# The tails of two graph convolutions: the first one's values made with nodes on the partitions, the second one's two activations of neighbouring chunks interleaved

## The chip, the cores and the metric

The kernel runs on one core of one Trainium2 chip. The metric is the time of one execution on the device, in microseconds (us).

## The reference, cut to what matters

The program is a graph network of four layers on 6,250 nodes and 106,250 edges (each layer: layer norm, ReLU, a graph convolution, added to x). The change touches only the third layer, in which a small network of its own computes a correction t for every node:

```python
h = jnp.ones((N, 1), x.dtype)
h = jax.nn.elu(spline_conv(h, row, col, basis, idx, stn1_w, stn1_b))   # [N, 64]  first convolution
h = jax.nn.elu(spline_conv(h, row, col, basis, idx, stn2_w, stn2_b))   # [N, 64]  second convolution
h = jax.nn.elu(h @ stn3_w + stn3_b)                                    # [N, 64]
t = h @ stn4_w + stn4_b                                                # [N, 3]
...
# spline_conv ends: out = segment_sum(msg); deg = segment_sum(1)
return out / jnp.maximum(deg, 1.0)[:, None] + b
```

Since the first convolution's input is all ones, its sum is one matrix product per node: the summed basis (125 values of a node) times stn1_w [125, 64]. ELU is computed as max(v, 0) + exp(min(v, 0)) - 1.

## The kernel before, in words

The kernel is a chain of phases. Each is a Block in which five instruction streams (SP, PE, ACT, DVE, POOL; that is SyncE, TensorE, ScalarE, VectorE, GpSimd) run side by side and wait for each other on semaphores. A Block ends when every stream has drained and met the others (in the trace: DRAIN and EVENT_SEMAPHORE on the Block's line), and `next_phase()` (L100) adds one more barrier. Nothing of the next phase starts earlier, its DMAs included. Nodes are 49 blocks (NB) of 128 nodes, grouped in 7 chunks (NCH) of 7 blocks; CHUNK is 896 nodes, HALF is 448. All tensors here are float32. PSUM is `ps`, 8 banks of 512 float32 on each partition.

**First tail.** `source_order_pass` (L1581, Block at L1617) goes over 880 tiles of 128 edges. For each tile POOL sends one indirect DMA (L1729) that scatters 128 records of 208 float32 into the DRAM table `rec_d`, from a ring of UB = 10 slots of G = 4 tiles; ACT fills a slot only when its last scatters have landed (L1699). PE and DVE sum the 125 basis values and a count of each node into `acc` [126, 6272], node along the free axis, the count in row 125. When the loop is done, POOL still has the ring to send and then waits for its landings (L1733). Beside that, the functions of `job_post_spline` (L1457) make the first convolution's values, one chunk after the other: PE multiplies `wt` and the selector `sel` (all ones in its row 125) with the chunk (two `product` calls, bank pairs 0 and 2), so that features lie on 64 partitions and the count is repeated on all of them; DVE takes max(count, 1) (L1507), its reciprocal (L1508), the quotient (L1509), and the two halves of ELU (`elu_of`, L1450 and L1451); ACT takes Exp (L1488); DVE adds up (L1453); PE turns the seven [64, 128] pieces so that nodes lie on partitions (L1306, bank 4); ACT copies them to `nodes` (L1491), and only then lets PE begin the next chunk (`s_out`). The `val`, `rc`, `low` and `hid` tiles are lent from the pass's `oh` and `basis`.

**Next phase.** `destination_order_pass` (L1883) begins with loads of weights (L2559) and of `rec_d` (L1910), the table that POOL has just filled.

**Second tail.** `post_stn` (L1514, Block at L1524) is a phase of its own, in which POOL issues nothing. Its input `rows` has nodes on the partitions. For each chunk in turn: PE turns seven blocks (L1537, into banks 0 and 1), DVE, ACT and DVE make ELU (L1450, L1451, L1559, L1453, into `hid`), PE multiplies by w3 (L1293, banks 4 and 5), DVE, ACT and DVE make ELU again into `hid2`, PE multiplies by w4 (L1552, bank 6), and DVE adds the last bias into `nodes` (L1577). There is one `low`, one `hid` and one `hid2`; PE turns the next chunk beside the second ELU.

Of the kernel before, what the change touches and what calls it, by code (L numbers as in the profile page):

```python
# [82 lines left out]
def build(nc, A, out, debug=None):  # L83
    ctx = ExitStack()
    with ctx:
# [574 lines left out]
        def column(ap):  # L660
            return ap.rearrange("(o a) -> o a", a=1)
# [785 lines left out]
        def elu_of(v, then, low, s_low, s_exp):  # L1447

            def elu(e, x, view, b, to, sem):
                nc.vector.tensor_scalar(view(low[:, :]), x, b, 0.0, ALU.add, ALU.min).then_inc(s_low, 1)  # L1450
                then(nc.vector.tensor_scalar(view(to[:, :]), x, b, 0.0, ALU.add, ALU.max))  # L1451
                v.wait_ge(s_exp, e + 1)
                nc.vector.scalar_tensor_tensor(out=to[:, :], in0=low[:, :], scalar=-1.0, in1=to[:, :],  # L1453
                                               op0=ALU.add, op1=ALU.add).then_inc(sem, 1)
            return elu

        def job_post_spline(c, acc, count_row, w1, b1, nodes, lent):  # L1457

            H = 64
            wt, bt = weight(c, "wt", count_row, H), weight(c, "bt", H, 1)  # L1460
            sel = weight(c, "sel", count_row + 1, H)
            rc, val, low, hid = lent
            s_w, s_z, s_mm, k, s_low, s_exp, s_hid, s_tr, s_out = (sem_in(c, n) for n in (
                "weights", "selector", "products", "chain", "low", "exp", "hid", "turned", "out"))
# [6 lines left out]
            def pe_start(pe):  # L1471
                pe.wait_ge(s_w, 32)
                pe.wait_ge(s_z, 1)
                nc.tensor.sem_inc(s_out, 1)

            def pe_chunk(pe, ch):
                pe.wait_ge(s_out, ch + 1)
                nc.tensor.sem_inc(tick, 1)
# [3 lines left out]
                nc.tensor.sem_inc(tick, 1)  # L1482
                turn(4, hid, H, s_tr)

            def act_chunk(act, ch):
                act.wait_ge(s_low, ch + 1)
                nc.scalar.sem_inc(tick, 1)
                nc.scalar.activation(low[:, :], low[:, :], ACT.Exp).then_inc(s_exp, 1)  # L1488
                act.wait_ge(s_tr, ch + 1)
                nc.scalar.sem_inc(tick, 1)  # L1490
                nc.scalar.copy(nodes[:, ds(ch * 7 * H, 7 * H)], ps[:, 4, 0:7 * H]).then_inc(s_out, 1)  # L1491

            def dve_start(v):
                select_row(c, sel[:, :], count_row).then_inc(s_z, 1)
                v.wait_ge(s_w, 32)

            def dve_chunk(v, ch):
                at = [0]

                def then(ins):  # L1500
                    at[0] += 1
                    ins.then_inc(k, 1)
                    v.wait_ge(k, 4 * ch + at[0])

                v.wait_ge(s_mm, ch + 1)
                nc.vector.sem_inc(tick, 1)
                then(nc.vector.tensor_scalar(split(rc[:, :]), halves(2, H), 1.0, None, ALU.max))  # L1507
                then(nc.vector.reciprocal(rc[:, :], rc[:, :]))  # L1508
# [5 lines left out]
        def post_stn(rows, b1, w_in, b_in, w_out, b_out, nodes):  # L1514

            H = 64
            with ExitStack() as c:
# [6 lines left out]
                with nc.Block() as block:  # L1524
# [9 lines left out]
                    def _(pe):  # L1534
# [1144 lines left out]
```

## Time and profile before

| what | value |
|---|---|
| time before, median of 3 runs | 11786.78 us (11779.63 to 11808.97) |
| the profiled execution | 11795.48 us, of which 11793.6 us are the span of the trace |
| POOL busy | 6775.0 us (57%) |
| PE, weight loads, DVE, ACT busy | 52%, 41%, 47%, 19% |
| TensorE clock granted, mean | 0.584 of full speed |

No engine is busy throughout: the phases have different limits, and a phase must be read by itself. In the rows below an instruction is given as: engine, line, operation, out<-in, form. "PEld" is the weight load of PE. A name with q (POOLq, SPq) is the engine's sequencer or DMA queue. The granted clock is a share of 2.4 GHz: 0.50 is the lower of its two levels, 1.2 GHz. A float32 matmul stands as two passes in the trace (the seven of L1552 are x14).

### The profile page before, as it was taken

What the parts mean: (1) busy time and instruction counts of PE and PEld (TensorE: products, weight loads), DVE (VectorE), ACT (ScalarE), POOL (GpSimd) and SP (SyncE); (2) the same over time, 40 slices, a digit from 0 to 9 for tenths busy, and PEclk for the clock granted to TensorE, in tenths of its full rate; (3) what the DMA queues carried; (4) which work ended last, traced back from release to release, by engine and by line L of the source; (5) the groups of instructions that cost most, each with busy time, mean ns of one, the idle gap of its engine ahead of it and who ended that gap; (6) DMA issues with size and microseconds to landing.
All of it is one profiled execution on the core that took longest, in us unless ns stands there. A gap on an engine that the chain in (4) does not pass through costs nothing. (4 is left out here: it accounts for less than half of the span.)

```text
span 11793.6 us, 174145 instructions
## 1 busy us (share of the span) xinstructions
PE 6097.0 (52%) x42047; PEld 4878.5 (41%) x42048; DVE 5490.5 (47%) x10617; ACT 2204.9 (19%) x6466; POOL 6775.0 (57%) x6936
## 2 busy tenths in 40 slices
PE   5200166665777756665534435555554555643535
PEld 1100045554777644445323324244444444432424
DVE  9200175555555578876734335721113333543425
ACT  0000034442333311110031220011111111122030
POOL 0777547774777767773462350067777777445070
PEclk9555587776555578875555555755555555555555
DMA  9940012222333311116744345580000111134454
GB/s 369 169 46 5 23 52 83 83 83 72 104 104 104 87 46 54 54 47 93 109 167 111 122 135 117 102 69 14 14 13 20 28 28 27 36 106 137 97 177 95
DMA packets 1401293, 1002.71 MB, mean 85 GB/s; under 512 B 950077, under 2 KB 1243772, under 8 KB 1383486
## 3 DMA queue, kind: packets, MB, share of 16 engines
q1 hardware_dynamic: 1006396, 578.07, 22.8%
q0 software_dynamic: 246144, 278.83, 7.7%
q10 hardware_dynamic: 148608, 144.19, 4.2%
q8 instruction: 54, 0.88, 0.0%
q14 instruction: 91, 0.74, 0.0%
HBM read 494.76 MB, written 546.25 MB: 88 GB/s over the span
## 5 line engine op out<-in xcount | busy, mean ns | idle before, releaser
L2500 POOL DMA_INDIRECT msg<-msg,idx x1792 | 1743.1, 973 | 592.9 <-issue 531.7
L976 POOL DMA_INDIRECT run_rows<-rec,idx x1088 | 1065.2, 979 | 1232.6 <-ACT rec L960 992.3
L2330 POOL DMA_INDIRECT cell<-rec,idx x944 | 931.3, 987 | 1007.6 <-ACT rec L2318 725.1
L665 DVE TENSOR_TENSOR oh<-iota_f,rd 128x512 bf16<-128x512 f32 (+1 forms) x1181 | 775.6, 690 | 1280.4 <-PE ps L2252 1015.3
L2052 POOL DMA_INDIRECT cell<-rec,idx x936 | 973.3, 1040 | 401.3 <-issue 284.6
L1729 POOL DMA_INDIRECT rec_d<-rec,idx x880 | 904.0, 1027 | 453.5 <-issue 267.0
L396 POOL DMA_INDIRECT rec_r<-sc_rec,sc_idx x832 | 816.4, 981 | 587.9 <-ACT sc_rec L387 307.0
L946 PE MATMUL ps<-planes,hot 128*128 x4352 | 474.9, 294 | 979.2 <-ACT rec L960 852.2
L931 DVE TENSOR_SCALAR hot<-loc,lane_c 128x512 bf16<-128x512 bf16 x1088 | 406.3, 387 | 958.4 <-PE ps L946 892.2
L946 PEld LDWEIGHTS ps<-planes,hot 128*128 128x128 bf16 x4352 | 363.8, 135 | 1090.7 <-issue 1042.6
L2480 PE MATMUL ps<-w_stn,hft 128*128 x1792 | 597.1, 491 | 405.3 <-ACT hft L2434 396.8
L2267 PE MATMUL ps<-h_rows,oht 128*128 x1888 | 450.9, 403 | 540.1 <-ACT oht L2274 539.7
L1042 PE MATMUL ps<-got,oh 128*128 128x33 bf16 x11328 | 561.7, 197 | 312.1 <-DVE oh L665 297.7
L2480 PE MATMUL ps<-w_conv,hft 128*128 x1792 | 436.8, 425 | 501.7 <-ACT hft L2434 501.7
L271 PE MATMUL ps<-mark,column 128*128 128x416 bf16 (+2 forms) x454 | 117.3, 375 | 1101.8 <-DVE mark L202 1096.1
L2267 PEld LDWEIGHTS ps<-h_rows,oht 128*128 128x128 f32 x1888 | 420.3, 327 | 633.6 <-issue 633.6
L2404 DVE TENSOR_REDUCE msg<-wy 128x256 f32<-128x1024 f32 (+1 forms) x448 | 525.8, 1174 | 274.2 <-DMA msg<-msg,idx 258.3
L1042 PEld LDWEIGHTS ps<-got,oh 128*128 128x128 bf16 x11328 | 483.5, 108 | 387.6 <-issue 332.5
L2480 PEld LDWEIGHTS ps<-w_conv,hft 128*128 128x128 f32 x1792 | 396.9, 326 | 587.8 <-issue 587.7
L2480 PEld LDWEIGHTS ps<-w_stn,hft 128*128 128x128 f32 x1792 | 414.5, 242 | 534.2 <-issue 465.5
L1970 PE MATMUL ps<-h,oht 128*128 x1872 | 459.0, 427 | 292.2 <-ACT rec L2034 292.2
L1759 PE MATMUL ps<-xgs,oht 128*128 x2640 | 402.7, 299 | 349.2 <-ACT rec L1674 348.8
(419 smaller groups left out, 13675.7 us busy)
## 6 DMA issues: line engine op xcount, KB each, us to landing
loc<-loc_s SPq DMA_DIRECT2D x136, 1024.0 KB
got<-run_rows SPq DMA_DIRECT2D x944, 112.0 KB
got<-rec_d SPq DMA_DIRECT2D x234, 416.0 KB
rec_d<-padd ACTq DMA_DIRECT2D x4, 12480.0 KB
rec_d<-padd ACTq DMA_DIRECT2D x4, 12064.0 KB
cin<-cell SPq DMA_DIRECT2D x224, 136.0 KB, 2.1
loc<-loc_d SPq DMA_DIRECT2D x236, 128.0 KB
cell<-rec,idx POOLq DMA_INDIRECT x1880
```

Of the source, the lines that this page charges most:

```text
L396: nc.gpsimd.indirect_dma_start(out=table, out_offset=bass.IndirectOffsetOnAxis(ap=s["idx"][:, n, g:g + 1], axis=0), in_=s["rec"][:, n, g, ...
L665: return nc.vector.tensor_tensor(oh, bcast(iota_f[:, :].unsqueeze(1), [P, G, P]), bcast(local.unsqueeze(2), [P, G, P]), ALU.is_equal)
L946: mm = nc.tensor.matmul(ps[:, m % RING, g * W:(g + 1) * W], hot[:, m % RING, g * P:(g + 1) * P], flat[:, ds(ids[m % HU] * W, W)], start=Tr ...
L976: nc.gpsimd.indirect_dma_start(out=out, out_offset=bass.IndirectOffsetOnAxis(ap=idx[:, u, m % HU:m % HU + 1], axis=0), in_=rec[:, m, :], i ...
L1042: mm = nc.tensor.matmul(sums[:, ds(at[n * G + g], AW)], oh[:, n, g, :], part[n][:, g, q * AW:(q + 1) * AW], start=False, stop=False)
L1729: nc.gpsimd.indirect_dma_start(out=rec_d, out_offset=bass.IndirectOffsetOnAxis(ap=idx[:, n, g:g + 1], axis=0), in_=rec[:, n, g, :], in_off ...
L2052: nc.gpsimd.indirect_dma_start(out=cells, out_offset=bass.IndirectOffsetOnAxis(ap=idx[:, n, g:g + 1], axis=0), in_=rec[:, n, g, :], in_off ...
L2267: mm = nc.tensor.matmul(ps[:, 2 + n % 2, g * W:(g + 1) * W], s["oht"][:, n % 2, g, :], nodes[:, ds(ids[g] * pitch, W)], start=True, stop=True)
L2330: nc.gpsimd.indirect_dma_start(out=cells, out_offset=bass.IndirectOffsetOnAxis(ap=idx[:, n, g:g + 1], axis=0), in_=rec[:, n, g, :], in_off ...
L2404: nc.vector.tensor_reduce(msg[:, n, :, 0:F], wy[:, n % 2, :, :, :].rearrange("p g c o -> p g o c"), AX.X, ALU.add).then_inc(s_msg, 1)
L2480: mm = nc.tensor.matmul(ps[:, 2 + banks * (n % 2) + col // 512, col % 512:col % 512 + rest * F], hft[:, n % 2, g, :], w, start=True, stop= ...
L2500: nc.gpsimd.indirect_dma_start(out=msgs, out_offset=bass.IndirectOffsetOnAxis(ap=idx[:, n, g:g + 1], axis=0), in_=msg[:, n, g, :], in_offs ...
```

## The change

In the first tail the stationary and the moving operand are exchanged: `acc` [126, 128 nodes] is loaded as the weights and one matrix `w_cnt` [126, 65] is moved, which holds stn1_w in columns 0 to 63 and a one for the count row in column 64. A block's result [128 nodes, 65] fills 65 columns of a bank, seven blocks fill a bank, and each of the seven chunks has a bank of its own (0 to 6). The count is then one column: max and reciprocal are taken of [128, 7]. The bias is added as a row `b_row`, loaded to all 128 partitions. Nothing is turned, and ACT copies nothing. PE waits for nobody between chunks; DVE makes the value of chunk q + 1 before it ends ELU of chunk q. The three streams are written out instead of looped. At the start of the phase SP's two small loads wait for DVE's memset of `w_cnt`, and DVE makes the selector column after these loads have landed.

In the second tail there are two `low` and two `hid`; PE turns chunk 1 at once and chunk ch + 2 after the product of chunk ch; DVE makes the first ELU of chunk ch + 1 between the parts of the second ELU of chunk ch.

```diff
         def job_post_spline(c, acc, count_row, w1, b1, nodes, lent):
             H = 64
-            wt, bt = weight(c, "wt", count_row, H), weight(c, "bt", H, 1)
-            sel = weight(c, "sel", count_row + 1, H)
-            rc, val, low, hid = lent
+            W = H + 1
+            w_cnt, b_row, rc = weight(c, "w_cnt", count_row + 1, W), sb_in(c, "b_row", [P, H]), sb_in(c, "rc", [P, NB])
+            low = [x.rearrange("p (b f) -> p b f", f=H) for x in lent]
+            def value(q):
+                return nodes[:, q * 7 * H:(q + 1) * 7 * H].rearrange("p (b f) -> p b f", f=H)
             def loads_sp(sp):
-                sp.dma_start(bt[:, :], column(b1)).then_inc(s_w, 16)
-                sp.dma_start(wt[:, :], w1).then_inc(s_w, 16)
+                sp.wait_ge(s_z, 1)
+                sp.dma_start(w_cnt[0:count_row, 0:H], w1).then_inc(s_w, 16)
+                sp.dma_start(b_row[:, :], bcast(b1.unsqueeze(0), [P, H])).then_inc(s_w, 16)
                 sp.wait_ge(s_w, 32)
-            def pe_chunk(pe, ch):
-                pe.wait_ge(s_out, ch + 1)
-                product(0, H, [(wt[:, :], moving(acc, count_row, ch))])
-                product(2, H, [(sel[:, :], moving(acc, count_row + 1, ch))], s_mm)
-                pe.wait_ge(s_hid, ch + 1)
-                turn(4, hid, H, s_tr)
-            def act_chunk(act, ch):
-                act.wait_ge(s_low, ch + 1)
-                nc.scalar.activation(low[:, :], low[:, :], ACT.Exp).then_inc(s_exp, 1)
-                act.wait_ge(s_tr, ch + 1)
-                nc.scalar.copy(nodes[:, ds(ch * 7 * H, 7 * H)], ps[:, 4, 0:7 * H]).then_inc(s_out, 1)
+            def pe_all(pe):
+                pe.wait_ge(s_w, 32)
+                pe.wait_ge(s_z, 2)
+                for q in range(NCH):
+                    for j in range(7):
+                        b = q * 7 + j
+                        mm = nc.tensor.matmul(ps[:, q, j * W:(j + 1) * W], acc[0:count_row + 1, b * P:(b + 1) * P], w_cnt[:, :],
+                                              start=True, stop=True)
+                    mm.then_inc(s_mm, 1)
+            def act_all(act):
+                for q in range(NCH):
+                    act.wait_ge(s_low, q + 1)
+                    nc.scalar.activation(low[q], low[q], ACT.Exp).then_inc(s_exp, 1)
             def dve_start(v):
-                select_row(c, sel[:, :], count_row).then_inc(s_z, 1)
+                nc.vector.memset(w_cnt[:, :], 0.0).then_inc(s_z, 1)
                 v.wait_ge(s_w, 32)
-            def dve_chunk(v, ch):
-                ...
-                then(nc.vector.tensor_scalar(split(rc[:, :]), halves(2, H), 1.0, None, ALU.max))
-                then(nc.vector.reciprocal(rc[:, :], rc[:, :]))
-                then(nc.vector.tensor_tensor(split(val[:, :]), halves(0, H), split(rc[:, :]), ALU.mult))
-                elu_of(v, then, low, s_low, s_exp)(ch, val[:, :], lambda a: a, bt[:, 0:1], hid, s_hid)
+                select_row(c, w_cnt[:, H:W], count_row).then_inc(s_z, 1)
+            def dve_all(v):
+                def mean(q):
+                    got = ps[:, q, 0:7 * W].rearrange("p (b f) -> p b f", f=W)
+                    mine = rc[:, q * 7:(q + 1) * 7]
+                    v.wait_ge(s_mm, q + 1)
+                    then(nc.vector.tensor_scalar(mine, got[:, :, H], 1.0, None, ALU.max))
+                    then(nc.vector.reciprocal(mine, mine))
+                    then(nc.vector.tensor_tensor(value(q), got[:, :, 0:H], bcast(mine.unsqueeze(2), [P, 7, H]), ALU.mult))
+                    then(nc.vector.tensor_tensor(value(q), value(q), bcast(b_row[:, :].unsqueeze(1), [P, 7, H]), ALU.add))
+                    nc.vector.tensor_scalar(low[q], value(q), 0.0, None, ALU.min).then_inc(s_low, 1)
+                def elu(q):
+                    then(nc.vector.tensor_scalar(value(q), value(q), 0.0, None, ALU.max))
+                    v.wait_ge(s_exp, q + 1)
+                    then(nc.vector.scalar_tensor_tensor(out=value(q), in0=low[q], scalar=-1.0, in1=value(q), op0=ALU.add, op1=ALU.add))
+                mean(0)
+                for q in range(NCH):
+                    if q + 1 < NCH:
+                        mean(q + 1)
+                    elu(q)
...
         def post_stn(rows, b1, w_in, b_in, w_out, b_out, nodes):
-                low, hid, hid2 = (sb_in(c, n, [H, CHUNK]) for n in ("low", "hid", "hid2"))
+                low, hid = ([sb_in(c, f"{n}{q}", [H, CHUNK]) for q in range(2)] for n in ("low", "hid"))
+                hid2 = sb_in(c, "hid2", [H, CHUNK])
...
                         turn_rows(0)
+                        pe.wait_ge(s_top, 1)
+                        turn_rows(1)
                         for ch in range(NCH):
                             pe.wait_ge(s_hid, ch + 1)
-                            product(4, H, [(w3[:, :], still(hid, H))], s_m3)
-                            if ch + 1 < NCH:
-                                turn_rows(ch + 1)
+                            product(4, H, [(w3[:, :], still(hid[ch % 2], H))], s_m3)
+                            if ch + 2 < NCH:
+                                pe.wait_ge(s_top, ch + 2)
+                                turn_rows(ch + 2)
                             pe.wait_ge(s_h3, ch + 1)
...
-                        for ch in range(NCH):
-                            v.wait_ge(s_turn, ch + 1)
-                            elu(2 * ch, flat, lambda a: a, bt[:, 0:1], hid, s_hid)
-                            v.wait_ge(s_m3, ch + 1)
-                            elu(2 * ch + 1, halves(4, H), split, b3[:, 0:1], hid2, s_h3)
-                            v.wait_ge(s_m4, ch + 1)
+                        def begin(e, to, x, view, b, top):
+                            nc.vector.tensor_scalar(view(e[:, :]), x, b, 0.0, ALU.add, ALU.min).then_inc(s_low, 1)
+                            nc.vector.tensor_scalar(view(to[:, :]), x, b, 0.0, ALU.add, ALU.max).then_inc(top, 1)
+                        def end(e, to, n, sem):
+                            v.wait_ge(s_exp, n)
+                            nc.vector.scalar_tensor_tensor(out=to[:, :], in0=e[:, :], scalar=-1.0, in1=to[:, :],
+                                                           op0=ALU.add, op1=ALU.add).then_inc(sem, 1)
+                        def first(ch):
+                            v.wait_ge(s_turn, ch + 1)
+                            begin(low[0], hid[ch % 2], flat, lambda a: a, bt[:, 0:1], s_top)
+                        first(0)
+                        v.wait_ge(s_top, 1)
+                        end(low[0], hid[0], 1, s_hid)
+                        for ch in range(NCH):
+                            more = ch + 1 < NCH
+                            if more:
+                                v.wait_ge(s_hid, ch + 1)
+                                first(ch + 1)
+                            if ch:
+                                keep(ch - 1)
+                            v.wait_ge(s_m3, ch + 1)
+                            v.wait_ge(s_h3, ch)
+                            begin(low[1], hid2, halves(4, H), split, b3[:, 0:1], k3)
+                            if more:
+                                v.wait_ge(s_top, ch + 2)
+                                end(low[0], hid[(ch + 1) % 2], 2 * ch + 2, s_hid)
+                            v.wait_ge(k3, ch + 1)
+                            end(low[1], hid2, 2 * ch + 3 if more else 2 * ch + 2, s_h3)
+                        keep(NCH - 1)
```

`keep(ch)` is the wait for w4's product and the addition that stood at L1576 and L1577. `w_cnt` is one tile; `select_row` (L1316) is unchanged.

## Rows read from the trace of the kernel before

**Rows 1.** The profile page: busy time of each engine.
```profile
...
PE 6097.0 (52%) x42047; PEld 4878.5 (41%) x42048; DVE 5490.5 (47%) x10617; ACT 2204.9 (19%) x6466; POOL 6775.0 (57%) x6936
```

**Rows 2.** Windows of the tails: us, busy of PE, PEld, DVE, ACT, POOL, clock, DMA.
```profile
...
2715.40:2847.10 131.70, 45.84 (x105) 16.81 (x105) 72.11 (x42) 10.38 (x14) 36.60 (x37) 0.63 0.03 9
5824.30:5925.00 100.70, 56.21 (x175) 33.99 (x175) 50.85 (x54) 14.58 (x15) 0.00 (x0) 0.50 0.00 0
```

**Rows 3.** Groups by line and form, 2715 to 2848 us.
```profile
...
L1508 DVE RECIPROCAL oh<-oh 64x896 f32<-64x896 f32 x7 | 40.2, 5745 | 0.2
...
L1450 DVE TENSOR_SCALAR basis<-oh,bt 64x896 f32<-64x896 f32 x7 | 4.7, 678 | 0.3
```

**Rows 4.** Timeline of the first tail: start, length, instruction, idle before it.
```profile
...
2715.44 3.25 PE L1293 MATMUL ps<-acc,wt 125*64 x4 [2.38 <-PEq L1474]
...
2732.21 1.25 POOL L1729 DMA_INDIRECT rec_d<-rec,idx  x1 [0.30 <-issue]
...
2762.19 0.97 POOL L1729 DMA_INDIRECT rec_d<-rec,idx  x1 [0.30 <-issue]
...
2846.52 0.53 ACT L1491 COPY h<-ps 128x448 f32 x1 [2.51 <-PE ps L1306]
2847.99 11.05 SPq L2559 DMA_DIRECT2D w_stn<-in_L_gnn_stn_w  x2
```

**Rows 5.** Sequencer events of the block at L1617 (ns: least, median, most).
```profile
...
L1617 POOLq EVENT_SEMAPHORE  x2: 17/17/17, 2847.1 to 2847.2; - x2
...
L1617 POOLq DRAIN  x1: 6601/6601/6601, 2764.5 to 2764.5; - x1
```

**Rows 6.** The POOL drain of three other blocks.
```profile
...
L2361 POOLq DRAIN  x2: 5287/5288/5290, 5311.1 to 10089.2; - x2
...
L2289 POOLq DRAIN  x1: 9208/9208/9208, 8925.2 to 8925.2; - x1
...
L569 POOLq DRAIN  x1: 19164/19164/19164, 1390.5 to 1390.5; - x1
```

**Rows 7.** Nearest instructions elsewhere: two of DVE by source, then PE and DVE by timeline.
```profile
...
L1439 DVE RECIPROCAL rc<-rc x3: 465/466/466, 4145.7 to 10448.1; 128x49 f32<-128x49 f32 x3
...
L1822 DVE TENSOR_TENSOR basis<-pair,hats x220: 678/679/745, 1582.8 to 2689.1; 128x500 f32<-128x500 f32 x110
...
6555.46 3.25 PE L1365 MATMUL ps<-v,hid 64*128 64x64 f32 x14
...
6558.64 1.75 PE L1293 MATMUL ps<-both_t,w 64*64 64x448 f32 x2
...
1572.17 5.29 DVE L1865 MEMSET acc<- 126x6272 f32 x1 [4.77 <-issue]
```

**Rows 8.** Window where L1365 ran.
```profile
...
6550.00:6600.00 50.00, 49.32 (x152) 29.59 (x153) 6.48 (x23) 11.95 (x13) 0.00 (x0) 0.50 0.00 0
```

**Rows 9.** Timeline of the second tail: its first chunk, and its last output.
```profile
...
5829.82 1.70 PE L1537 MATMUL ps<-ident,sums 128*64 128x128 f32 x7 [9.55 <-DMA b<-in_L_gnn_stn_b]
...
5832.71 1.13 DVE L1451 TENSOR_SCALAR hid<-ps,bt 64x896 f32<-64x896 f32 x1
...
5833.87 1.08 DVE L1453 SCALAR_TENSOR_TENSOR hid<-low,hid 64x896 f32<-64x896 f32 x1
...
5835.01 3.24 PE L1293 MATMUL ps<-hid,w 64*64 64x448 f32 x4 [3.49 <-DVE hid L1453]
...
5838.29 1.14 DVE L1450 TENSOR_SCALAR low<-ps,b 64x896 f32<-64x896 f32 x1 [3.33 <-PE ps L1293]
...
5840.53 1.08 DVE L1453 SCALAR_TENSOR_TENSOR hid<-low,hid 64x896 f32<-64x896 f32 x1
...
5841.66 3.15 PE L1552 MATMUL ps<-w,hid 64*128 64x4 f32 x14 [1.78 <-DVE hid L1453]
5844.85 0.19 DVE L1577 TENSOR_TENSOR t_nm<-ps,b 128x28 f32<-128x28 f32 x1 [3.24 <-PE ps L1552]
...
5924.66 0.18 DVE L1577 TENSOR_TENSOR t_nm<-ps,b 128x28 f32<-128x28 f32 x1 [3.23 <-PE ps L1552]
```

More of the change, by code:

```diff
@@ L1445, in _ @@
                         then(nc.vector.tensor_tensor(x_nm[:, :, :], x_nm[:, :, :], val, ALU.add))
[L1447 to L1455, printed above, removed]
@@ L1512, in job_post_spline @@
-            return dict(sp=loads_sp, pe_start=pe_start, pe_chunk=pe_chunk, act_chunk=act_chunk, dve_start=dve_start, dve_chunk=dve_chunk)
+                select_row(c, w_cnt[:, H:W], count_row).then_inc(s_z, 1)
+            def dve_all(v):
+                then = chain(v, k)
+                def mean(q):
[16 more added lines that the diff above has]
+                    elu(q)
@@ L1557, in _ @@
                         for e in range(2 * NCH):
+                            to = low[0 if e == 0 or (e % 2 == 1 and e < 2 * NCH - 1) else 1]
                             act.wait_ge(s_low, e + 1)
-                            nc.scalar.activation(low[:, :], low[:, :], ACT.Exp).then_inc(s_exp, 1)
+                            nc.scalar.activation(to[:, :], to[:, :], ACT.Exp).then_inc(s_exp, 1)
                     @block.vector
@@ L1569, in _, with keep @@
                         v.wait_ge(s_w, 80)
-                        elu = elu_of(v, then, low, s_low, s_exp)
-                        for ch in range(NCH):
+                        def begin(e, to, x, view, b, top):
[6 more added lines that the diff above has]
+                        def first(ch):
                             v.wait_ge(s_turn, ch + 1)
-                            elu(2 * ch, flat, lambda a: a, bt[:, 0:1], hid, s_hid)
-                            v.wait_ge(s_m3, ch + 1)
-                            elu(2 * ch + 1, halves(4, H), split, b3[:, 0:1], hid2, s_h3)
+                            begin(low[0], hid[ch % 2], flat, lambda a: a, bt[:, 0:1], s_top)
+                        def keep(ch):
                             v.wait_ge(s_m4, ch + 1)
@@ L1602, in source_order_pass @@
                      "basis", "summed", "added", "filled", "consts", "away"))
-                room = [x[0:64, :, :, :].rearrange("p r g w -> p (r g w)") for x in (oh, basis)]
-                post = job_post_spline(c, acc, KW, w1, b1, nodes,
-                                       [x[:, h * CHUNK:(h + 1) * CHUNK] for x in room for h in range(2)])
+                room = [x[:, :, :, :].rearrange("p r g w -> p (r g w)") for x in (oh, basis)]
+                post = job_post_spline(c, acc, KW, w1, b1, nodes, [room[q // 4][:, q % 4 * HALF:(q % 4 + 1) * HALF] for q in range(NCH)])
                 shift = {-4.0: 0, 1.0: 1, -3.0: 2, 2.0: 3, -2.0: 4, 4.0: 5}
@@ L1717, in _ @@
                         spans(act, body)
-                        with act.Fori(0, NCH) as ch:
-                            post["act_chunk"](act, ch)
+                        post["act_all"](act)
                     @block.gpsimd
@@ L1778, in _ @@
                         pe.wait_ge(s_fill, NT * UB + 2)
-                        post["pe_start"](pe)
-                        with pe.Fori(0, NCH) as ch:
-                            post["pe_chunk"](pe, ch)
+                        post["pe_all"](pe)
                     @block.vector
@@ L1879, in _ @@
                         v.wait_ge(s_cast, NT * UB)
-                        with v.Fori(0, NCH) as ch:
-                            post["dve_chunk"](v, ch)
+                        post["dve_all"](v)
         def destination_order_pass(rd, acc, nodes, F, cells, load_weights):
```

23 lines of the change are left out of this document (5 added, 18 removed).

## The prediction

> **What bounds the kernel now.** I read the page first: no engine is busy throughout, and the largest share, GpSimd's 57%, is an average over phases [rows 1]. So the question is which stream ends each of the two phases that the change touches. The windows give the stakes [rows 2]: the first tail is 131.7 us long, the second phase 100.7 us, and no engine is busy for more than 72 of the one or 56 of the other. Both are chains of waits. Together they are 232.4 us, 2.0% of the time, and no more than that is at stake.
>
> *First tail.* The timeline has PE's first product at 2715.44 and ACT's last copy at 2846.52 [rows 4]; seven chunks in series, 18.8 us each. The groups say what fills a chunk: the reciprocal of 896 elements on 64 partitions, 5.745 us, is the largest piece [rows 3]. But another stream runs beside it. POOL sends its ring until 2762.19 [rows 4], and the Block's events tell how that stream ends: its last wait is over and its DRAIN begins at 2764.5, and this DRAIN lasts 6.60 us, to 2771.1 [rows 5]. Now that is hidden: the last stream arrives, and POOL's event of the barrier follows, at 2847.1 [rows 5]. The reader is to see that POOL's drain is the floor of this phase, and that it lies 76.0 us below the present end.
>
> *Second tail.* One chunk by the timeline [rows 9]: product 5835.01, min 5838.29, last part of ELU 5840.53, w4's product 5841.66, bias 5844.85; the last bias at 5924.66 is (5924.66 - 5844.85) / 6 = 13.30 us per chunk. PE waits while DVE and ACT make an ELU, and DVE while PE multiplies. POOL issues nothing there, so no floor lies near.
>
> **First tail, part by part.** Removed for each chunk: the product with the selector, DVE's 5.745 us reciprocal, seven turns, ACT's copy (0.53 us), and PE's wait for it. Added:
>
> - PE: seven float32 matmuls of 65 columns on loads of 128, 14 passes. The nearest row is L1365, 64 columns on 64 rows, 14 passes in 3.25 us, with the next product 3.18 us after its start, where the granted clock was 0.50, the lower level [rows 8]. Seven chunks: 22.3 us. They wait for nobody.
> - DVE: max of [128, 7] and its reciprocal, at most the 0.47 us that 49 elements took [rows 7] each; a product, an addition and L1453's operation over 448 elements, at most 0.68 us each, what 500 elements took [rows 7]; min and max over 448, at most the 0.68 us that 896 took [rows 3]. Upper sum 0.94 + 2.04 + 1.36 = 4.3 us. Scaled to 448 elements and 7, it is about 0.3 + 1.8 + 0.7 = 2.8 us. I add 0.4 for chained waits and take 3.2 us, the same as PE's.
>
> So DVE's last chunk ends at about 2715.4 + 7 x 3.2 + 3.5 = 2741, at the upper bound 2715.4 + 3.2 + 7 x 4.3 = 2749. Both are before 2764.5. What ends the phase is POOL. The gain stops at POOL's floor, and PE's and DVE's exact costs are then worth nothing, as long as a chunk takes less than (2771.1 - 2718.6) / 7 = 7.5 us.
>
> What the change does to POOL itself: in the first chunk one scatter lasted 1.25 us instead of 0.97, beside DVE's last ELU operation [rows 4], and there was one such scatter in each of the two full chunks before POOL ended. I take that as DVE holding POOL up, 0.28 us for about 2.4 us of DVE work that has two SBUF inputs or runs at the fast rate (L1450's 0.68 us for 896 [rows 3], L1451 the same, L1453's 1.08 us). The new code has some 1.9 us of that in each of seven chunks, 13.3 us: 13.3 x 0.28 / 2.4 = 1.6 us, less the 0.56 us that go, is +1.0 us. Bounds: 0, and all 13.3 us. *The Trainium skill, SBUF — State Buffer, section "Who interferes with whom", calls the ports that the two engines share an exclusive lock which blocks the loser for the whole instruction, for tensor_scalar in its fast mode and for two SBUF inputs. The rows agree in kind, with 0.28 us of 1.08. By the rule in full the sum would be 12.3 us worse; it is a rival below.*
>
> The drain: 6.60 us here, with as many scatters and as large ones after the change. Elsewhere it lasted 5.29, 9.21 and 19.16 us [rows 6], so it is no constant; I keep 6.60, bounds 5.29 and 19.16. At the head of the phase the selector column now follows the loads (the wait behind which DVE's memset of `acc` stands is 4.77 us [rows 7]): about 0.1 us later for it, and everything of this POOL-paced pass is behind it. The bias load writes 128 rows instead of 64; I cost it at nothing, up to 0.5 us. POOL's end: 2771.1 + 1.0 + 0.1 = 2772.2. Gain 2847.1 - 2772.2 = **74.9 us**. The next phase's loads, issued 0.9 us after the barrier [rows 4, 5], move up with it. They need POOL's table, so could not have started earlier.
>
> **Second tail.** The same instructions in another order. Per chunk, from the start S of the operation that completes `hid2` [rows 9]: w4's product at S + 1.13; the w3 product of the next chunk is now ready and follows on PE 3.18 us later [rows 7], S + 4.31; min of its result 3.28 us later, S + 7.59; max, then the two closing additions at 2.24 us and one more operation of 1.08 us behind: S + 7.59 + 2.24 + 1.08 = S + 10.9. First ELU, turns and the bias lie inside PE's 6.4 us. So 10.9 us against 13.30. The ends: in chunk 0 PE makes the second turn first (it starts at 5833.9 when max is ready, and lasts 1.7 us [rows 9]), which puts the product 0.6 us later, and the added first-ELU operation 1.08 us more: S(1) is 5840.53 + 1.6 = 5842.1. Five periods of 10.9, then a last one without the next chunk's operation, 9.8: S(7) = 5906.5 and the last bias 4.32 us behind (5844.85 - 5840.53), 5910.8. Gain 5924.66 - 5910.8 = **13.9 us**. Bounds: 0.5 us per period either way, 11 and 17. PE's share: its 6.4 us per period are at the lower clock, 0.50 [rows 2].
>
> **Sum.** 74.9 + 13.9 = 88.8 us. The profiled execution took 11795.48 us: 11706.7. It stands 8.7 us above the median of the runs shown; against that median, 11786.78 - 88.8 = **11698 us**, 0.75% faster. A change under 0.3% (35 us) could not be told from none.
>
> **Rivals.**
>
> 1. *The drain shrinks or stretches* when it alone ends the phase. A POOL that issued nothing drains at once, and the rows with scatters spread from 5.29 to 19.16 [rows 6]. 19.16 gives 11711 us. *The Trainium skill, VectorE: DVE Perf Modes, section "The DRAIN you can't avoid", tells of DRAINs of about 12 ns on all engines at the ends; were POOL's that short with nothing behind it, the time would be 11691 us.* The rows speak against it: in four blocks with scatters, none under 5.2 [rows 5, 6]. Chance 0.08 for the long one, 0.03 for none.
> 2. *DVE locks POOL out in full*: 12.3 us more, 11710 us. For: the scatter of 1.25 us [rows 4]. Against: it was 0.28 us per chunk so far. Chance 0.07.
> 3. *DVE's chunk stays the end of the first tail*, a chunk over 7.5 us, because chained small operations cost more than the rows show. At 10 us a chunk the end is 2789: 11715 us. Chance 0.04.
> 4. *TensorE's clock rises in the second tail*, since it is busy 56 of 87 us instead of 101. Products would take half: about 2.7 us less per chunk, 11682 us. Against: where L1365 stands PE was busy for 49.3 of 50 us and the clock was 0.50 [rows 8]. Chance 0.04.
> 5. *The interleaving gives nothing*, because PE's turn or a wait falls into the period: 11712 us. Chance 0.04.
> 6. *Slower.* The head of the phase: DVE's memset of `acc` stands behind the loads, which now wait for DVE first and of which one is a broadcast to 128 partitions. POOL paces the pass, so each microsecond there is paid in full. The wait is 4.77 us now [rows 7]; it decides from 89 us on; at twice that, 178 us, the time would be 11876. Nothing among the rows is near. Chance 0.02. In between, at no measurable change: 0.03.
>
> The forecast has what is left, 0.65, with 11688 to 11706 us from its bounds and the spread of the runs before (7 us below the median, 22 above). The range reaches from rival 4's side to past rivals 1, 2, 3 and 5: 11681 to 11720. Faster by over 0.3%: 0.95; same 0.03; slower 0.02.
>
> **What would show it.** In the first tail: POOL's DRAIN on the Block's line is the last and the barrier follows it at about 2772; DVE's last closing addition lies near 2741, 14 passes of PE take about 3.2 us; scatters over 0.97 us are few. In the second: 10.9 us from w4's product to w4's product, the last bias 86 to 87 us after the phase's begin instead of 100.4. Wrong would make it: another stream than POOL last in the first, a drain far from 6.6, or later phases that give back what comes early.

## The result, and the profile after

The changed kernel takes 11734.55 us (median of 6 runs, 11720.64 to 11748.36), the kernel before 11807.06 us (median of 6 runs on the same chip, 11779.63 to 11813.3; the first three of them had the median 11786.78 that the prediction used). The ratio is 0.9945, 95% interval 0.9931 to 0.9958: 0.55% or 72.5 us faster. The prediction had 11698 us, a range to 11720, and a gain of 88.8 us. The measured time lies outside the range. The profiled execution took 11736.98 us, of which 11734.4 are the span, 59.2 less than the span of before.

Both tails first. Timeline of the first tail after:

```profile
...
2708.08 20.01 PE L1470 MATMUL ps<-w_cnt,acc 126*128 126x65 f32 x98 [1.78 <-DVE acc L1887]
...
2710.31 0.17 DVE L1491 TENSOR_SCALAR rc<-ps 128x7 f32<-128x7 f32 x1 [2.29 <-PE ps L1470]
...
2717.77 1.15 POOL L1758 DMA_INDIRECT rec_d<-rec,idx  x1 [0.31 <-issue]
...
2732.83 0.63 DVE L1500 SCALAR_TENSOR_TENSOR h<-basis,h 128x448 f32<-128x448 f32 x1
...
2755.26 0.97 POOL L1758 DMA_INDIRECT rec_d<-rec,idx  x1 [0.30 <-issue]
2765.09 9.84 SPq L2585 DMA_DIRECT2D w_stn<-in_L_gnn_stn_w  x2
```

Sequencer events of its block (ns: least, median, most):

```profile
...
L1647 POOLq EVENT_SEMAPHORE  x2: 17/17/17, 2764.2 to 2764.3; - x2
...
L1647 PEldq DRAIN  x1: 4070/4070/4070, 2724.1 to 2724.1; - x1
L1647 ACTq DRAIN  x1: 604/604/604, 2731.4 to 2731.4; - x1
...
L1647 DVEq DRAIN  x1: 17/17/17, 2733.7 to 2733.7; - x1
...
L1647 POOLq DRAIN  x1: 6601/6601/6601, 2757.6 to 2757.6; - x1
```

The seven chunks that took PE and ACT until 2846.52 [rows 4] are done by DVE 25.4 us after PE's first product. DVE's drain begins at 2733.7, but the barrier comes at 2764.2: 2757.6 + 6.60. POOL is now the last stream, and its drain has the length of before to the nanosecond [rows 5]. The first product of w4 to the last, and the last bias, in the second tail after:

```profile
...
5793.40 3.15 PE L1552 MATMUL ps<-w,hid 64*128 64x4 f32 x14 [2.66 <-DVE hid L1578]
...
5796.48 3.24 PE L1293 MATMUL ps<-hid,w 64*64 64x448 f32 x4
...
5799.76 1.14 DVE L1573 TENSOR_SCALAR low<-ps,b 64x896 f32<-64x896 f32 x1 [2.99 <-PE ps L1293]
...
5801.89 2.07 DVE L1578 SCALAR_TENSOR_TENSOR hid<-low,hid 64x896 f32<-64x896 f32 x2
...
5804.01 3.15 PE L1552 MATMUL ps<-w,hid 64*128 64x4 f32 x14 [2.66 <-DVE hid L1578]
...
5846.47 3.15 PE L1552 MATMUL ps<-w,hid 64*128 64x4 f32 x14 [4.29 <-DVE hid L1578]
```

From product to product it is 10.61 us, against the 13.30 of before [rows 9]. PE's clock stayed where it was. Windows of the first tail and of the whole second phase, with columns as in rows 2:

```profile
...
2708.00:2764.30 56.30, 20.01 (x98) 19.82 (x98) 20.93 (x50) 4.04 (x7) 36.95 (x38) 0.51 0.08 22
...
5774.60:5859.90 85.30, 55.81 (x175) 34.02 (x175) 50.01 (x54) 14.57 (x15) 0.00 (x0) 0.50 0.00 1
```

The lengths of phases can be read from POOL's barrier events on each Block's line, as in rows 5. All that differ by over 2.5 us between the two profiled executions:

| phase | before, us | after, us | difference |
|---|---|---|---|
| source pass with the first tail | 1280.9 | 1203.6 | -77.3 |
| second tail | 100.7 | 85.3 | -15.4 |
| sum of messages and ids (scatters of L1123) | 321.0 | 357.3 | +36.3 |
| third of four phases at L1006 | 245.1 | 253.2 | +8.1 |
| a phase before the pass (L569) | 1105.6 | 1101.0 | -4.6 |
| L2289 before, L2315 after | 1239.2 | 1235.4 | -3.8 |
| first phase at L912 | 371.9 | 369.3 | -2.6 |

The rest adds up to 0.1. The two tails gave 92.7 us; what is missing was given back later, in phases whose source did not change. For the largest piece there is one row, a single scatter (the 114th of 236) that lasted 38.89 us where its neighbours last 0.97:

```profile
...
5534.59 0.97 POOL L1123 DMA_INDIRECT run_ids<-acc_nm  x1 [0.30 <-issue]
5545.02 38.89 POOL L1123 DMA_INDIRECT run_ids<-acc_nm  x1 [9.46 <-issue]
5584.22 0.97 POOL L1123 DMA_INDIRECT run_ids<-acc_nm  x1 [0.30 <-issue]
```

Before, the longest of the same 236 took 1.50 us:

```profile
...
L1123 POOL DMA_INDIRECT run_ids<-acc_nm x236: 971/976/1499, 5475.5 to 5791.9; - x118
```

The idle time of about 9 us ahead of it is no part of the loss: before, 9.12 us stand at the same place. POOL ends this phase, so the long scatter counts; DVE, the next stream, is through 34 us earlier, so without it the phase would have been some 35 us shorter, not 38:

```profile
...
L2209 DVEq DRAIN  x1: 17/17/17, 5710.0 to 5710.0; - x1
...
L2209 POOLq DRAIN  x1: 876/876/876, 5744.4 to 5744.4; - x1
```

The +8.1 us are spread over the 59 turns of a loop. The window of that phase and DVE's main group, before and after (the columns of a group are busy us, mean ns | idle us before):

```profile
...
10848.00:11093.10 245.10, 142.15 (x2840) 121.83 (x2840) 154.22 (x241) 0.00 (x0) 0.00 (x0) 0.50 0.55 111
...
L665 DVE TENSOR_TENSOR oh<-iota_f,rd 128x512 bf16<-128x512 f32 x236 | 151.9, 688 | 85.3 <-PE ps L1042 85.2
```

```profile
...
10779.30:11032.50 253.20, 150.28 (x2840) 122.35 (x2840) 149.96 (x241) 0.00 (x0) 0.00 (x0) 0.50 0.53 107
...
L665 DVE TENSOR_TENSOR oh<-iota_f,rd 128x512 bf16<-128x512 f32 x236 | 147.7, 687 | 97.8 <-PE ps L1042 97.5
```

The counts and the granted clock are the same, and no DVE operation is longer. DVE waits 12.3 us more for PE, and PE's busy time is 8.1 us longer at the same number of matmuls. So PE's stream itself runs slower. The starts of the single matmuls in the trace show that it does so at one place of its code: a turn of the loop has 48 matmuls of L1042, and from the start of the 5th to that of the 6th it is 118 ns on average where it was 28, and from the 6th to the 7th 112 where it was 44; the first 12 matmuls of the 59 turns took 34.3 us in all instead of 26.2, the other 36 as long as before within 1 us. What had changed for PE was only where its code lies: in the built program its stream has 14,347 instructions instead of 14,195, and the 152 new ones all stand ahead of this phase.

### The profile page after: what moved, and what is told of

The parts are those of the page before. It is cut to its first block and busy times, and to the rows that moved or that the text cites. A ratio compares the mean times of both kernels' runs of the same rounds, so it can differ in the third digit from the quotient of the medians.

```text
span 11734.4 us, 174003 instructions
## 1 busy us (share of the span) xinstructions
PE 6071.7 (52%) x42040; PEld 4886.1 (42%) x42041; DVE 5431.0 (46%) x10625; ACT 2195.1 (19%) x6459; POOL 6800.9 (58%) x6936
## 5 line engine op out<-in xcount | busy, mean ns | idle before, releaser
L1042 PE MATMUL ps<-got,oh 128*128 128x33 bf16 x11328 | 571.0, 197 | 313.8 <-DVE oh L665 297.6
L1042 PEld LDWEIGHTS ps<-got,oh 128*128 128x128 bf16 x11328 | 486.3, 109 | 396.0 <-issue 339.4
```

The costliest lines, as they stand in the source:

```text
L1042: mm = nc.tensor.matmul(sums[:, ds(at[n * G + g], AW)], oh[:, n, g, :], part[n][:, g, q * AW:(q + 1) * AW], start=False, stop=False)
```

## The experiments

The kernel before, which took 11,807 us in the first timing, takes 13,433 us beside e1 to e4 (chip number 15 on record), 13,426 beside e5 to e8 (number 5), 13,583 beside e9 to e12 (number 7) and 13,559 beside e13 to e16 (number 5 again). Below, "the first chip" is that of the first timing, and "the other chips" are these. But the number 5 stands for two times that are 1% apart, and the first chip has no number on record: whether the chip itself or another condition of a timing makes the difference is not shown. Each run has the ratio to the kernel before that was timed beside it. Phase lengths come from one profile each. For the length of the source pass, three profiles of the changed kernel's pass at 13,560 to 13,580 us give 1469.2, 1473.2 and 1474.7, so a few microseconds there mean nothing; those of the third L1006 phase agree within 1 us.

**Kernel before, and kernel after, once more.**

> The kernel before, unchanged, for a second profile. In the first pair of profiles the two changed phases gained 77.4 and 15.4 us, but the phase that sums the messages (Block at L2183) grew by 36.2 us, with one POOL scatter of L1123 that lasted 38.89 us. Theory A (the long scatter comes by chance, in either kernel): the source pass is 1281 us and the second tail 100.7 us long again, while the phase at L2183 can be 321 or some 355 us here as well; some of the executions lie 30 us and more above others. Theory B (the change brings the long scatter about, by where it puts the phase in time or its code in memory): 321 us here, and no scatter of L1123 above 2 us.

> The changed kernel, unchanged, for a second profile. Both theories: source pass 1203.6 us, second tail 85.3 us. Theory A: the phase that sums the messages is 321 us as often as 357, and over enough executions the gain is near 92 us. Theory B: 357 us again, one scatter of L1123 near 39 us at the same place in its row of 236, and the gain stays near 72 us.

e1: 13434.85 us, ratio 1.0001 (0.9991 to 1.0011). e2: 13325.5, 0.9913 (0.9896 to 0.9929), 107.7 us faster. The source pass went from 1553.2 to 1447.5 us (-105.7), which is more than on the first chip, and the second tail from 100.8 to 85.6. The third L1006 phase lasted 253.3 instead of 244.3 us: this loss is there again. No scatter of L1123 was longer than 2.5 us.

The source pass ends in another way on these chips. Events of the block in e2:

```profile
...
L1647 POOLq DRAIN  x1: 6601/6601/6601, 3037.0 to 3037.0; - x1
...
L1647 DVEq DRAIN  x1: 17/17/17, 3060.6 to 3060.6; - x1
```

POOL is through at 3043.6, and DVE at 3060.6 sets the end. The groups of POOL over the pass tell why, first in the changed kernel on the first chip, then in e2:

```profile
...
L1758 POOL DMA_INDIRECT rec_d<-rec,idx x880 | 902.1, 1025 | 453.4 <-issue 267.1 <-ACT rec L1704 186.3
```

```profile
...
L1758 POOL DMA_INDIRECT rec_d<-rec,idx x880 | 913.1, 1038 | 676.1 <-ACT rec L1704 425.3 <-issue 250.8
```

On the first chip 185.4 of the 186.3 us that POOL waits for ACT stand before the first scatter; then it hardly waits, and the ring is nearly full when the pass's loop ends: 38 scatters follow. In e2 192.9 of 425.3 us stand before the first, and 232 us of waiting fall into the pass: the ring is nearly empty at the end, and so POOL has no backlog behind which seven chunks could hide: it sends its last scatter 5.3 us after PE's first product, against 47.2 us on the first chip. On these chips the gain is not cut at POOL's floor.

**Each tail alone.** e3 is the changed kernel with `post_stn` as before, e4 the kernel before with the new `post_stn`.

> Only the first tail changed, post_stn as before. Both theories: source pass 1204 us (77 us less), second tail 100.7 us, so 77 us faster without the message phase. Theory B, if the first tail is what brings the long scatter about: 77 - 36 = 41 us faster than before, with the scatter near 39 us; if not, 77. Theory A: 77 us, or 41 by chance.

> Only the second tail changed (post_stn), the first as before. It runs after the phase with the long scatter, so it can bring it about only by the layout of the code. Both theories: source pass 1281 us, second tail 85.3 us, 15.4 us less. Theory B by layout: the long scatter here too, 15 - 36 = 21 us slower than before. Theory A: 15 us faster, give or take the chance.

e3: 13342.68 us, 0.9926 (0.9909 to 0.9942), -90.5; source pass 1449.5, second tail 100.8, third L1006 phase 252.8. e4: 13416.74, 0.9984 (0.9974 to 0.9993), -16.5; 1553.0, 85.3, 243.4. The two add up to 107.0, and both together gave 107.7. The loss in the L1006 phase comes with the first tail's change alone, which stands ahead of that phase by some 8,000 us and has no code in it.

**PE's code put back, all streams' code put back.** e5 adds PE instructions that do nothing but count, behind the new products: 152 and 104 make 256, so that the later code lies where it lay before, modulo 256 instructions:

```diff
                         post["pe_all"](pe)
+                        for _ in range(104):
+                            nc.tensor.sem_inc(tick, 1)
```

e6 does so for every stream: 201 such increments on DVE, 8 on ACT, 8 on POOL, 6 on SP.

> The changed kernel with 104 semaphore increments added on PE behind its products of the first tail. The change made PE's code 152 instructions longer; with these it is 256 longer, so all later code of PE lies at the old place modulo 256 instructions. In every profile with the new first tail the summing phase that is third of four (Block at L1006) took 253 us, in every one with the old tail 243.4 to 245. Theory L (layout of PE's code): 245 us again, the rest as in the changed kernel, so 8 us faster than it. Theory T (it is the data, the time or another stream that moved): 253 us. The increments cost PE about 5 us behind POOL's scatters and the phase nothing.

> The same for all five streams: the increments bring the later code of PE and DVE to 256 instructions behind the old place, and that of ACT, POOL and SP to the old place. Theory L': layout of DVE's or another stream's code counts: 245 us here, and 253 in the run with PE's alone. Theory L: 245 us in both. Theory T: 253 us in both. With layout as before, the gain over the kernel before should be the two tails' own: 77 + 15 = 92 us where POOL ends the source pass.

e5: 13323.21 us, 0.9921 (0.9905 to 0.9938); the third L1006 phase is back at 244.1, the one at L2119 at 353.3 instead of 355. e6: 13332.15, 0.9929 (0.9912 to 0.9946); 245.2 and 353.1, but its source pass lasts 1459.6 instead of e5's 1447.1, since the 201 increments lie on DVE's end, the last one there. The position of DVE's, ACT's, POOL's and SP's code adds nothing to these two phases. The expectation that the increments cost the source pass nothing did not hold: in e5 PE's drain, at 3060.9, is the last, 1.5 us behind DVE's, and it is so in e9 and e14 too. In the total, e5's 10 us are less than its interval; the phase is what shows it, and e14 repeats it.

**DVE's share, and the next phase's head.** e7 and e12 make each quotient four times, 21 more operations of 0.62 us, 13 us with their gaps:

```diff
-                    then(nc.vector.tensor_tensor(value(q), got[:, :, 0:H], ..., ALU.mult))
+                    for _ in range(4):
+                        then(nc.vector.tensor_tensor(value(q), got[:, :, 0:H], ..., ALU.mult))
```

e8 lets the first loads of `rec_d` in `destination_order_pass` go ahead of the weights:

```diff
-                        load_weights(sp, s_w)
-                        with sp.Fori(0, NTD) as i:
-                            ...
+                        load(0)
+                        load_weights(sp, s_w)
+                        with sp.Fori(1, NTD) as i:
+                            load(i)
```

> The changed kernel, with the quotient of each chunk of the first tail written four times instead of once: 21 more operations of DVE of 0.65 us, 13.7 us. Theory P (POOL's ring, its landings and its drain end the pass, DVE has some 24 us to spare): the source pass is as long as in the changed kernel on the same chip, 0 us. Theory D (DVE's chain ends it): 13.7 us longer. In the first pair of profiles POOL was last by far; in the profiles on the chip of the second call, where the whole kernel took 13433 us, DVE was last at 3060.6 and POOL's drain had ended at 3043.6. So: 0 us if the time of before is near 11800, 13.7 us if it is near 13400.

> The changed kernel, and in the next phase SP issues the first six loads of rec_d ahead of the two loads of weights, which nobody reads in that phase (they held SP for 9.8 us, and DVE's first one-hot began 24 us after the barrier). If the phase is paced by POOL from its first scatter on, it is shorter by what the first scatter comes earlier: 10 to 20 us faster than the changed kernel, in the phase at L1926 alone. If the weights' many small packets only delay later loads instead, 0.

e7: 13333.91 us, 0.9934 (0.9918 to 0.9951). DVE ends its source pass, 26.8 us after POOL's drain is over:

```profile
...
L1648 POOLq DRAIN  x1: 6601/6601/6601, 3040.0 to 3040.0; - x1
...
L1648 DVEq DRAIN  x1: 17/17/17, 3073.4 to 3073.4; - x1
```

So DVE is on the path there. The length of the pass, 1459.9 against e5's 1447.1, gives +12.8, as expected, but that the number fits is luck: PE's first product came 8.1 us later in e7's pass than in e5's, and in e5 DVE began 11.1 us after it instead of 3.4. From PE's first product to the end of the phase e7 took 39.5 us; e8, whose first tail is that of the changed kernel, took 30.9. e8: 13311.75, 0.9914 (0.9898 to 0.9931); the destination pass lasted 1455.7, against 1464.7, 1464.5 and 1460.1 in e5 to e7. SP's queue of e8:

```profile
...
3061.47 2.77 SPq L1936 DMA_DIRECT2D got<-rec_d  x6
3064.29 16.07 SPq L2590 DMA_DIRECT2D w_stn<-in_L_gnn_stn_w  x2
3073.54 0.97 POOL L2083 DMA_INDIRECT cell<-rec,idx  x1 [35.04 <-ACT rec L2065]
```

The first scatter comes 14 us after the phase's begin, in e2 31 us. Of those 17 us, 4.4 to 9.0 are left at the end of the phase, and 10 to 20 were expected.

**Both mends together.** e9 is the changed kernel with e5's and e8's edits; e10 and e11 are the kernels before and after, e12 is e7 once more, all on one chip.

> The changed kernel with both mends: the 104 increments that bring PE's later code back to its old place modulo 256 instructions, and the weights of the next phase loaded behind its first six loads. By the profiles so far 9 + 2 us and 10 us: 21 us faster than the changed kernel, in the phases at L1006 (third, 244.5 us), L2119 (353 us) and L1926 (10 us less), and nowhere else.

> The kernel before once more, for the phase that sums the messages and for the end of the source pass. If this is a chip where it takes about 11800 us, theory A (the long scatter of L1123 comes by chance in either kernel) and theory B (the change brings it) are tried again: A allows 321 or about 357 us here, B only 321. POOL's last wait of the source pass 1198 us after the phase began, its drain 6.60 us. If it takes about 13430 us: 598 us, and POOL's drain ends 120 us ahead of the phase.

> The changed kernel once more. Where before takes about 11800 us: source pass 1203.6 us, POOL's drain last; second tail 85.3; third phase at L1006 253; theory A: phase of the messages 321 or 357, theory B: 357. Where before takes about 13430 us: source pass 1447 with DVE last, no long scatter.

> The changed kernel with the quotient of each chunk of the first tail written four times, for the case that this chip has POOL last in the source pass. Theory P there: source pass 1204 us as in the changed kernel, 0 us longer, DVE's last operation 13.7 us nearer to the end. Where before takes about 13430 us: 12.4 us longer, as in the first run of it.

e9: 13459.11 us, 0.991 (0.9893 to 0.9926). e10: 13583.62, 1.0001 (0.9991 to 1.0011). e11: 13475.74, 0.9918 (0.9901 to 0.9935). e12: 13481.07, 0.9925 (0.9909 to 0.9942). By phases, e9 against e11: destination pass 1470.8 against 1487.7 (-16.9), third L1006 phase 243.5 against 253.2 (-9.7), L2126 352.8 against 355.3 (-2.5), source pass 1479.1 against 1474.7 (+4.4: the 104 increments end after DVE here). In the medians it is 16.6 us less than e11, in the direction expected, though the two intervals overlap. e12's source pass was 7.9 us longer than e11's, where 12.4 was expected; its first product came 7.9 us earlier in the pass, and from there to the end it was 44.2 us against 28.5. The other case of this test, a chip with POOL last, where more DVE work was to cost nothing, did not come up.

**The long scatter, and the code's position once more.**

> The kernel after once more, for the ids phase. In its first profile one scatter of L1123 lasted 38.89 us instead of 0.97 and that phase 357.3 us instead of 321.0; eight later profiles, four of them of the kernel with this first tail, had none. By chance: no long one here, and where the chip runs the kernel before at about 11800 us the phase is 321 us and the difference to before about 72 to 110 us. Of the change: a long one beside the gap after scatter 112, 30 to 40 us, wherever the phase takes about 321 us.

> PE's code put back to its old place modulo 256 instructions. If the third of the L1006 phases costs by code position on every chip: it lasts 244 to 245 us instead of 253, and the phase of the messages to come after it 353 instead of 355, 10 us less than after in all. If code position has to do with the long scatter too, none is seen here and one is in e13. If neither: as e13 within 0.05%.

> The kernel before, one look. By chance: its ids phase lasts either the 321 us of before's first profile or 598 us, depending on the chip, and a long scatter may stand here as well as in e13. If the long one comes with the change: none here.

> The kernel after, one more look on the same chip. If the long scatter comes with the change it stands in e13 and here alike, at the same number of scatter; if by chance, in neither or in one of the two.

e13: 13440.97 us, 0.9918 (0.9904 to 0.9931). e14: 13433.75, 0.9908 (0.9893 to 0.9924). e15: 13549.99, e16: 13448.78, one execution each. None has a scatter of L1123 over 2.5 us, and the phase lasts 598 to 599 us in all four. The question whether the scatter of 38.89 us comes with the change is therefore not answered: in all sixteen runs this phase takes 597 to 599 us, whatever the kernel, and POOL does not end it (in e1 POOL's drain begins at 6573.2 and DVE's, the last, at 6857.7). The third L1006 phase is 252.6 and 252.5 in e13 and e16, 244.3 in e14 and 244.7 in e15. Its window and DVE's group in e14, beside e13's:

```profile
...
12422.80:12667.10 244.30, 141.44 (x2838) 121.86 (x2840) 149.77 (x241) 0.00 (x0) 0.00 (x0) 0.50 0.55 111
...
L665 DVE TENSOR_TENSOR oh<-iota_f,rd 128x512 bf16<-128x512 f32 x236 | 147.5, 686 | 89.1 <-PE ps L1042 88.9
```

```profile
...
12420.20:12672.80 252.60, 149.13 (x2838) 121.93 (x2840) 149.74 (x241) 0.00 (x0) 0.00 (x0) 0.50 0.53 107
...
L665 DVE TENSOR_TENSOR oh<-iota_f,rd 128x512 bf16<-128x512 f32 x236 | 147.4, 686 | 97.5 <-PE ps L1042 97.2
```

DVE's wait for PE and PE's busy time fall by 8 us, with the same matmuls, and the two long steps in each turn of the loop are gone (28 and 43 ns, where e13 has 118 and 112). That 104 instructions which do nothing mend it shows that the position of PE's code is the cause. In the total e14 is 7.2 us under e13, with overlapping intervals. Only these two positions were tried: that 256 is the number that counts is a guess which one case fits, and what happens at that place is open.

## Why the prediction was off

**First tail, floor of POOL: right.** Predicted 74.9 us, measured 77.3. POOL's DRAIN is last, of 6.60 us as taken, and the barrier follows 1203.6 us after the phase's begin. DVE's chunks began 2.9 to 3.3 us apart, for the 3.2 worked out, and DVE's last addition ends 25.4 us after PE's first product (predicted 25.6). PE's chunk took 20.01 / 7 = 2.86 us, not 3.2. The 2.4 us more than predicted are POOL's loop, which ended 1.4 us earlier after the phase's begin (less than profiles of one kernel differ), and the 1.0 us that stood for contention: five scatters of 1.05 to 1.15 us, 0.5 us in all, and the old ones of before gone. *The rule of the Trainium skill, SBUF — State Buffer, "Who interferes with whom", taken in full was 12.3 us; DVE worked 20.93 us beside POOL, and the longest scatter was 0.18 us over the common one. The section has the case of two SBUF inputs only against a GpSimd instruction that reads SBUF, which the prediction left out. The full 12.3 us did not come.* The drain was neither of rival 1's values. But the prediction's "in four blocks with scatters, none under 5.2" was a choice of rows: in the same trace POOL's drain lasted 3.98 us at L912 (272 scatters) and 0.88 at L2183 (236), so the lower bound of 5.29 had no ground. *The Trainium skill's section "The DRAIN you can't avoid" (VectorE: DVE Perf Modes) gives its 12 ns for the DRAINs of a program's start and end, not for those of a block; here DVE's 17 ns is near it, POOL's 6601, PE's 4070 and ACT's 604 are not.* That POOL's stream is the floor on this chip is read from the order of the drains in one profile; no run with more or less DVE work was made there.

**Head of the phase: right.** DVE's memset of `acc` begins 0.4 us later after the phase's begin, of the predicted 0.1, and the first scatter 0.5 us. Rival 6 needed 89.

**Second tail: right, a little low.** 15.4 us for 13.9: the period was 10.61 and not 10.9, since nearly every step of the chain was a little shorter: 3.08 us and not 3.18 from w4's product to w3's, 2.13 and not 2.24 from min to the closing additions, 1.04 and 1.08 for each of these and not 1.08 and 1.13. The clock stayed at 0.50, so rival 4 did not come; rivals 3 and 5 neither.

**The step that failed is one that the sum had put at nothing: that all later phases stay as they are.** The text named "later phases that give back what comes early" as what would make it wrong, but gave it neither a price nor a chance. Two things stood against it, and only the first is shown to come with the change. The new code of PE shifts the code behind it, which costs 8 to 10 us in the third L1006 phase and at L2119; it was seen in each profile of a kernel with the first tail's change, and went in each in which PE's code was put back (e5, e6, e9, e14). And in the profiled execution one scatter took 36 us more. Without it the phase would have been some 35 us shorter, and the profiled execution, 59.2 us shorter in its span than that of before, would have been some 94 us shorter, at about 11702 us. That is 19 us under the fastest of the other five, 11720.64. Whether those had such a scatter can't be seen.

**The base.** Of the 36.6 us between 11698 and 11734.55, 20.3 are the kernel before itself: the median of three runs was 11786.78, that of six 11807.06. The working took 8.7 us off for a profiled execution that stood above the median; the later runs lay above both. The other 16.3 us are the gain's: 92.7 from the tails, less 9.9 for PE's code (8.1 and 1.8), leaves 82.8, of which 72.5 were measured. The last 10 us are not explained; a long scatter in some runs would, and so would the spread of the six runs (27.7 us after, 33.7 before). Either of the two parts, the base's 20.3 or the gain's 16.3, would alone have left the time within the range: 11807.06 - 88.8 is 11718.3, and 11786.78 - 72.5 is 11714.3.

**On the other chips** the gain was 0.8 to 0.9% (107 to 118 us). The step "PE's and DVE's exact costs are worth nothing" does not hold where POOL has no backlog at the end of the pass: there DVE's drain is the last (PE's, where the increments were added), and the 13 us of more DVE work made the stretch from PE's first product to the end longer, by 8.6 us (e7 against e8) and 15.7 us (e12 against e11). The step was read from one profile, and is a property of the conditions of that timing as much as of the kernel.

## What to carry to other kernels

Find the stream that ends next behind the one you shorten, drain included: it gave the gain of the first tail to within 2.4 us. Then ask on which paces it depends, since on another chip another stream was next. Written-out code shifts everything behind it in its engine's stream, and here that cost 8 to 10 us in phases nobody had touched: put such a term into the range, and look at the phases that the change does not touch before you explain the ones it does. And take the base from as many runs as the gain is small: three were 20 us off here.

## What the runs showed that was not expected

- The position of PE's code: 252.5 to 253.7 us against 243.4 to 245.2 us for the same loop, nine profiles each. The other three phases of L1006, whose code is written out anew, did not change by more than profiles of one kernel differ.
- One indirect DMA of 38.89 us among 236 of 0.97, seen in one of eighteen profiles. Its cause is open.
- POOL's DRAIN at the end of the source pass was 6.60 us in all eighteen profiles.
- The same kernel took 11,807 us in the first timing and 13,426 to 13,583 us on the chips of the experiments. The phase of sums and ids took 321 against 598 us, the third L1006 phase of the kernel before 244 to 245 on all of them. The kernel before shows where a part of the time goes: over the loop of its source pass two groups of PE's matmuls stood idle for 0.2 us in the first timing, and in e1 for 324 us, without waiting for anything that the profile shows ("issue"); their whole idle time was 359 and 540 us. The granted clocks of the whole executions are near each other, 0.584 and 0.571. First the kernel before in the first timing, then e1:

```profile
...
L1759 PE MATMUL ps<-xgs,oht 128*128 x2640 | 402.7, 299 | 349.2 <-ACT rec L1674 348.8 <-issue 0.2
L1766 PE MATMUL ps<-oh,basis 128*126 128x128 f32 x1760 | 342.6, 357 | 10.1 <-DVE acc L1860 10.0
```

```profile
...
L1759 PE MATMUL ps<-xgs,oht 128*128 x2640 | 400.3, 305 | 362.8 <-issue 176.9 <-ACT rec L1674 164.9 <-ACT oht L1668 19.8
L1766 PE MATMUL ps<-oh,basis 128*126 128x128 f32 x1760 | 384.7, 356 | 176.9 <-issue 147.3 <-DVE acc L1860 25.1
```

  What holds PE there was not tried.
- On the slower chips DVE began its first chunk late. In e2 PE's products start at 3029.44 and DVE's first operation at 3038.39, 8.95 us later, against 2.23 on the first chip; its stream has nothing else to do in between:

```profile
...
3029.44 8.58 PE L1470 MATMUL ps<-w_cnt,acc 126*128 126x65 f32 x39 [8.22 <-DVE acc L1887]
...
3038.39 0.17 DVE L1491 TENSOR_SCALAR rc<-ps 128x7 f32<-128x7 f32 x1 [9.01 <-remote]
```

In the other profiles there it was 6.2 to 11.1 us, or 3.4 to 3.7 with 7.0 to 8.8 us instead of 3.1 (in e12 instead of 5.1) between the first two chunks; only e7 had neither. What it waits for was not tried.
